# A rank behind the next batch's first scores, its counts in 16 bits, a norm ahead of a context half, and a semaphore of its own for the router's matrix

## The reference, cut to what matters

```python
x = x + tanh(g_xattn) * (gelu(layernorm(x) @ ctx.T) @ ctx)       # per batch
xf = layernorm(x)                                                  # the "second norm"
scores = softmax(xf @ gate_w)                                      # gate_w: the router's matrix, 512 x 8
top_scores, top_idx = top_k(scores, 2)
for each expert e:  xs = scale[:, e] * xf                          # scale: top_scores, 0 elsewhere
    y += (silu(xs @ w1[e]) * (xs @ w3[e])) @ w2[e]
x = x + tanh(g_ffn) * y
```

## Time and profile before

| | us |
|---|---|
| median of 3 runs | 810.37 |
| lowest and highest | 801.66, 811.13 |
| the profiled execution | 810.19 |
| its span | 808.4 |

### The profile page before, as it was taken

The page is one execution under the profiler, slowest core; times in us unless marked ns, Lnnn a source line. Parts: engine busy times, 40 slices in busy tenths (PEclk is TensorE's granted clock), DMA queues, the critical chain, the costliest instruction groups (busy, mean ns, idle before and its releaser), DMA issues.

```text
span 808.4 us, 17787 instructions
## 1 busy us (share of the span) xinstructions
PE 679.2 (84%) x4670; PEld 471.4 (58%) x4671; DVE 427.3 (53%) x1281; ACT 465.0 (58%) x775; POOL 424.2 (52%) x662
## 2 busy tenths in 40 slices
PE   0598897988898897888878734999999999999992
PEld 0576676876677776767767632555554555555551
DVE  2247667567676677676766772333334333333331
ACT  3777787587686877876867421443443443443441
POOL 2333356456457555764675652455555555555552
PEclk9999999699999999989999956999999999999997
DMA  5325545525444354355441222467566666566564
GB/s 160 103 77 171 147 133 138 151 90 136 141 138 114 115 170 122 123 147 170 121 121 49 72 73 66 79 107 127 106 116 115 108 113 117 106 108 124 99 114 75
DMA packets 51344, 94.30 MB, mean 117 GB/s; under 512 B 17024, under 2 KB 25344, under 8 KB 51312
## 3 DMA queue, kind: packets, MB, share of 16 engines
q1 hardware_dynamic: 34096, 60.02, 26.9%
q0 software_dynamic: 16400, 33.89, 22.8%
q10 hardware_dynamic: 816, 0.02, 0.1%
HBM read 61.89 MB, written 32.01 MB: 116 GB/s over the span
## 4 chain that ended last, share of the span: by engine, by line
DMA 29%; issue 16%; PE 14%; POOL 12%; DVE 7%; ACT 5%; POOLq 1%; DVEq 1%; ACTq 0%; SPq 0%; another core or an unknown queue 0%
DMA out_rows<-ctx_raw,meta 24%; PE bank L1173 4%; PE bank L1304 3%; PE bank L1161 2%; POOL route_table L470 2%; DMA ctx_raw<-xf_rows,meta 2%; ACT squares L571 2%; DVE stats L796 2%; POOL ex L462 2%; PE bank L1314 2%; DMA w_raw<-in_L_ffn_w 2%; POOL out_rows L540 1%; POOL exp_f L437 1%; DVE xf L871 1%; POOL ve L429 1%
## 5 line engine op out<-in xcount | busy, mean ns | idle before, releaser
L1304 PE MATMUL bank<-w,ctxT 128*128 x756 | 174.5, 381 | 0.0
L540 POOL DMA_INDIRECT out_rows<-ctx_raw,meta x63 | 99.3, 1577 | 123.9 <-DMA out_rows<-ctx_raw,meta 109.4
L1173 PE MATMUL bank<-ctx_part,a_part 125*112 125x512 f16 x576 | 145.5, 401 | 10.1 <-DVE a_part L828 10.1
L1161 PE MATMUL bank<-xnT,ctxT 128*125 128x224 f16 x1152 | 131.6, 275 | 4.7 <-DVE xnT L849 2.3
L1161 PEld LDWEIGHTS bank<-xnT,ctxT 128*125 128x125 f16 x1152 | 122.5, 148 | 6.2 <-issue 4.7
L1304 PEld LDWEIGHTS bank<-w,ctxT 128*128 128x128 f16 x756 | 74.3, 98 | 76.1 <-issue 1.6
L609 ACT ACTIVATE ctxT<-bank 128x1000 f16<-128x1000 f16 x96 | 95.4, 1014 | 22.2 <-PE bank L1119 22.0
L1173 PEld LDWEIGHTS bank<-ctx_part,a_part 125*112 125x112 f16 x576 | 75.7, 137 | 54.7 <-issue 8.3
L773 ACT ACTIVATE ctxT<-bank,cols 128x256 f32<-128x256 f32 x63 | 29.9, 474 | 112.6 <-issue 102.4
L1314 PE MATMUL bank<-w2s,ctxT 128*128 x378 | 91.9, 379 | 1.3 <-DVE ctxT L1079 1.3
L528 POOL DMA_INDIRECT ctx_raw<-xf_rows,meta x66 | 65.4, 991 | 29.5 <-issue 19.2
(11 more groups left out here) (142 smaller groups left out, 1078.1 us busy)
## 6 DMA issues: line engine op xcount, KB each, us to landing
ctx_raw<-in_ctx SPq DMA_DIRECT2D x48, 448.0 KB
w_raw<-in_L_ffn_w SPq DMA_DIRECT2D x24, 512.0 KB
x<-in_x SPq DMA_DIRECT2D x16, 448.0 KB, 5.6
out_rows<-x SPq DMA_DIRECT2D x16, 448.0 KB, 4.7
xf_rows<-xf SPq DMA_DIRECT2D x16, 448.0 KB
ctx_raw<-in_ctx SPq DMA_DIRECT2D x48, 52.0 KB
meta<-route_table SPq DMA_DIRECT2D x66, 1.0 KB
ctx_raw<-xf_rows,meta POOLq DMA_INDIRECT x66
```

Source lines behind the costliest of these rows:

```text
L540: g.indirect_dma_start(out=out, out_offset=bass.IndirectOffsetOnAxis(ap=meta[n][:, 0:1], axis=0), in_=y_sb[n % 2], in_offset=None, compute ...
L1161: ins = t_.matmul(dst, ctxT[u][:, hc * KD + k, c * CS:c * CS + CR], xnT[u][:, hx, k, :], start=j == 0, stop=j == KD * len(PARTS) - 1)
L1173: ins = t_.matmul(O_ps[t][0:TT, :], a_part[ha][:, c, t * TT:(t + 1) * TT], ctx_part[u][hc][:, c, :], start=c == 0 and (ha, hc) == PARTS[0] ...
L1304: ins = t_.matmul(H_ps[u][:, :], rows, w, start=m == 0, stop=m == KD * len(PARTS) - 1)
```

## The change

Four edits.

1. `small_loaded` becomes two semaphores, `g_loaded` for the gates and `gate_loaded` for the router's matrix. ScalarE waits only for the gates, TensorE only for the matrix.
2. `lower`, M and R are float16 instead of float32, and a second, 16-bit array of ones is made at the start.
3. On TensorE `rank(i-2)` no longer ends the step of batch i. It is the second item of the step of batch i+1, right behind the first `scores` (the last batch keeps one more at its old place). On VectorE `route_pos` moves along: from the end of a step to the place ahead of the first `a_low` of the next.
4. On VectorE the middle of a step is reordered. It was: routing scores, second context half, weight's low part, second `a_low`, `norm2`. It is: weight's low part, second `a_low`, `norm2`, second context half, routing scores.

```diff
-        lower = sb("lower", [TT, TT])
+        lower = sb("lower", [TT, TT], F16)
...
+        ones16 = sb("ones16", [TT, P], F16)
...
-        M = sb("M", [TT, 2, E])
-        R = sb("R", [TT, 2, E])
+        M = sb("M", [TT, 2, E], F16)
+        R = sb("R", [TT, 2, E], F16)
...
-        small_loaded = sem("small_loaded")
+        g_loaded, gate_loaded = sem("g_loaded"), sem("gate_loaded")
...
+            seq.done(g.memset(ones16[:, :], 1.0))
...
             for n, g in enumerate((g_xattn, g_ffn)):
-                a.dma_start(g_raw[:, n:n + 1], g.rearrange("(a n) -> a n", a=1).to_broadcast([P, 1])).then_inc(small_loaded, 16)
-            a.dma_start(gate[:, :, :], gate_w.rearrange("(k p) e -> p k e", p=P)).then_inc(small_loaded, 16)
-            act.wait_ge(small_loaded, 48)
+                a.dma_start(g_raw[:, n:n + 1], g.rearrange("(a n) -> a n", a=1).to_broadcast([P, 1])).then_inc(g_loaded, 16)
+            a.dma_start(gate[:, :, :], gate_w.rearrange("(k p) e -> p k e", p=P)).then_inc(gate_loaded, 16)
+            act.wait_ge(g_loaded, 32)
...
                 if not u and later(i, 1):
                     stats2(j)
+                if later(i, 3):
+                    route_pos(i - 3, w, h - 1 - w)
                 a_low(i, u, 0)
...
                     context_factors(i + 1, w)
-                if later(i, 3):
-                    route_scores(i - 3, w)
-                if not last:
-                    context_low(i + 1, w, 1)
                 late_matrix(weight_low, i, u, h)
                 a_low(i, u, 1)
                 if later(i, 1):
                     norm2(j)
+                if not last:
+                    context_low(i + 1, w, 1)
+                if later(i, 3):
+                    route_scores(i - 3, w)
...
                     xnT_low(i + 1, i * 4 + 3, w, 1)
-                if later(i, 2):
+                if last:
                     route_pos(i - 2, u, h - 1)
...
-            pe.wait_ge(small_loaded, 48)
+            pe.wait_ge(gate_loaded, 16)
...
                 scores(i, u, 0)
+                if later(i, 3):
+                    rank(i - 3)
...
                     trans_ctx(i + 1, w, 5)
-                if later(i, 2) and not last:
-                    rank(i - 2)
```

More of the change, by code:

```diff
@@ L1203, in rank @@
                 t_.matmul(rk_ps, lower[:, :], M[:, :, :].rearrange("p t e -> p (t e)"), start=True, stop=False)
-                t_.matmul(rk_ps, ones[0:TT, 0:TT], R[:, :, :].rearrange("p t e -> p (t e)"), start=False, stop=True).then_inc(rank_made, 1)
+                t_.matmul(rk_ps, ones16[:, 0:TT], R[:, :, :].rearrange("p t e -> p (t e)"), start=False, stop=True).then_inc(rank_made, 1)
             trans_ctx(0, 0, 0)
@@ L1270, in _ @@
             pe.wait_ge(pos_read, B)
-            t_.matmul(cnt_ps, ones[0:TT, :], R[:, 0, :], start=True, stop=True).then_inc(counts_made, 1)
+            t_.matmul(cnt_ps, ones16[:, :], R[:, 0, :], start=True, stop=True).then_inc(counts_made, 1)
             pe.wait_ge(w_split, 3 * E)
@@ L1347 @@
 POOL_IDENT = 6
-POOL_START = 16
+POOL_START = 17
 _INS = ['x', 'ctx_1024', 'g_xattn', 'g_ffn', 'L0_ffn_gate_w', 'L0_ffn_w1', 'L0_ffn_w2', 'L0_ffn_w3']
```

## The result

The changed kernel takes **824.08 us**, median of four runs (820.33 to 825.87); the kernel before took 806.01 beside it (four runs, 800.43 to 811.13). The ratio is 1.0233 [1.0187, 1.028]: 1.9 to 2.8% slower, where I had forecast 821 us and 1.3% (and had given 0.76 to a change of less than 2%, which this interval neither shows nor rules out). The profiled execution took 825.45 us with a span of 823.5, against 810.19 and 808.4.

A forecast was written before the change was run, and what follows sets the result against it. VectorE, though busy only 53%, was taken to set the pace where nothing covers its added work. On 810.19 us: -6.2 + 6 x 1.2 + 6 x 1.1 + 2.9 = +10.5, so 820.7, forecast 821; eight in ten 807 to 831.

The forecast's parts named there:

- Part 1: Start-up: with its own semaphore for the matrix, ScalarE's tanh and what follows come 6.2 us earlier; other end 4.4.
- Part 2: Odd batch's end: moving the rank leaves TensorE's stall, now waiting for xnT; gain 0.06 us per odd batch.
- Rival D: TensorE's clock falls more often in longer idle pieces, one more fall per pair of batches; 831 us, slower, chance 0.19.
- Part 3: Positions behind the residual delay VectorE's chain and TensorE's logits; +1.2 us per odd batch, 0 per even batch.
- Part 4: Even batch: later routing scores delay the next statistics, +1.1 us; xf stall shrinks by 1.2, xn stall grows to 3.0.
- Part 5: Last batch: positions and later routing scores delay GpSimd's sends and exponential, so the last residual comes 2.9 us later.
- The sign that I had set: Time from one even batch's scores to the next's: 53.8 us before, 56.1 forecast; 54 or less would refute it.
- B: Rival: only the start counts, the later edits cost nothing; 804 us, chance 0.15.
- A: Rival: one of the two per-batch costs, the even one, is covered by other waits; 812 us, chance 0.12.
- C: Rival: TensorE's own order is the bound, so its waits for R and xf vanish; 785 us, chance 0.04.

The follow-up runs named there:

- e1: Kernel before with only the semaphore split between gates and router's matrix; 803.83 us, ratio 0.9929 to the kernel before.
- e6: Changed kernel with odd batches' positions back in the even batch's end and routing scores back ahead of the weight's low part; 808.55 us, ratio 1.0037 to the kernel before.
- e2: Changed kernel with the rank (still 16-bit) and all positions back at the end of a batch; 811.31 us, ratio 1.0049 to the kernel before.
- e10: e6 plus 14 idle matmuls on TensorE in the idle piece at each odd batch's end; 808.39 us, ratio 1.0003 to the kernel before.
- e3: Changed kernel with the routing scores put back ahead of the weight's low part; 821.77 us, ratio 1.0163 to the kernel before.
- e5: Changed kernel with only the odd batches' positions moved back to the end of the even batch ahead; 813.71 us, ratio 1.0123 to the kernel before.
- e12: Kernel before with the split semaphore plus 14 idle matmuls ahead of the rank at its old place; 798.13 us, ratio 0.9887 to the kernel before.
- e4: Changed kernel plus 20 idle matmuls ahead of the odd batches' logits; 821.18 us, ratio 1.0136 to the kernel before.
- e8: e6 with even batches' late weight half put last on ScalarE and VectorE, second context half moved ahead; 796.44 us, ratio 0.9824 to the kernel before.

## Why the prediction was right, and where its sizes were off

It had the sign and the mechanism, and 824.08 lies well inside 807 to 831. That it lies so near to 821 is luck in part. I added +10.5 us to a profiled execution of 810.19, and the kernel before had a median of 806.01 beside the change. The change itself cost 18 us by medians and 2.3% by ratio (1.9 at least), where I had 10.5 us and 1.3%; in the two profiles it is 11.9 up to the expert part and 15.1 in all. So the sum was too small, and a base that was 4 us too high made up for part of it.

**Part 1, the start: -6.2 forecast, -6.38 in the profile, -5.7 for the edit alone.** The context rows were there in time, which had been the doubt.

**Part 2, the rank: the stall renamed, gain 0.06.** As forecast: 3.28 to 3.29 us where it was 2.64 and the rank. In how often slow scores follow little changed, four of six in both profiles (three in e1, five in the change's second profile). Whether the longer piece has a price of its own stays open. In e6 slow scores followed six times of six, and each odd batch took 29.3 us, 1.5 more than the four of e2 with fast scores; the filler (e10) took just that 1.5 us off each odd batch. But behind the same piece slow scores followed three times of six in e3 and three of four in e5. Over all profiles it is 30 of 40 against 9 of 15, which is 0.15 of 1.5 us per odd batch, 1.4 us in all, if it is no accident. Rival D named the lengthening, without a price of its own. The rank alone was not moved in a run.

**Part 3, the positions: +1.2 forecast per odd batch, +2.87 in the pair shown (22.07 to 24.94), +2.3 on the mean of six.** This is the term that was mis-sized. Both halves of the mechanism are there. The block stands unbroken between residual and a_low, and the logits wait for pos_read, 2.23 us where I had reckoned 2.6. What I priced at nothing was the clock behind that wait. The logits end late by the wait and by their own 0.7 us, and the attention takes 5.35 us instead of 2.79; it was slow in all six odd batches (4.46 to 5.35), in five of six in the second profile. I had supposed that a slower TensorE is hidden in its own waits, since VectorE sets the pace. For the kernel before that holds: its odd batches with fast scores at the end took 27.9 us with an attention of 4.31 and 27.6 with one of 2.79, and VectorE never waited for a there. In e12 the same attention was slow in four (4.47 to 4.48) of the five odd batches with fast scores, and they took 27.8 to 27.9 us where the one with a fast attention took 27.7. In the change the attention starts 1.8 us later behind the residual (344.65 - 340.70 against 340.78 - 338.65) and is longer still, and the cover is used up. VectorE's next inputs pass through TensorE and ScalarE. ScalarE and VectorE in that odd batch:

```profile
350.62 1.91 ACT L611 ACTIVATE ctxT<-bank 128x1000 f16<-128x1000 f16 x2 [5.76 <-PE bank L1123]
```

```profile
355.55 0.68 DVE L830 SCALAR_TENSOR_TENSOR a_part<-a_f,factors,a_part 125x448 f16<-125x448 f32 x1 [1.89 <-ACT a_part L625]
```

ScalarE waits for the transposes behind the slow attention, and VectorE waits 1.89 us for ScalarE, as it does in five of the six odd batches (1.88 to 1.89). About 1.6 us of the excess gets through, and e4 gave back just that (31.1 to 29.5). So this is rival D's mechanism, in the odd batches, on top of the forecast. The Trainium skill's rule that I had weighed ("TensorE: Matmul & The Clock Gate", section "HAM oscillation — how this bites in real kernels") says that the price of waits for data between short bursts is paid in every repetition. The traces agree nearly for the odd logits, 17 of 18 in the change's two profiles and e3, and less for the scores at an odd batch's end, four of six in the change and 30 of 40 over all.

**Part 4, the even batch: +1.1 forecast, +1.25 in the pair.** Statistics, batch and next norm are late by that much, and e3 gave 1.0 back on that chain. The split into 0.8 for xf and 3.0 for xn did not hold in this pair: TensorE waited 1.86 and 1.23, since a slow attention between them (4.44 us) had used up the second wait. Elsewhere the waits for xn reached 2.9. On the mean of the five even batches it is only +0.4, because the profile before has one even batch of 31.1 us; against e1's 26.7 it is +0.6.

**Part 5, the last batch: +2.9 and one even term of 1.1 forecast from the totals of batch 14 on, 3.4 measured** (12.9 less 9.6). The sends wait 2.91 us for the routing scores and the exponential follows them, as foreseen:

```profile
464.26 1.06 POOL L472 DMA_INDIRECT route_table<-route,pos_i  x1 [2.91 <-DVE tok L916]
...
469.19 2.94 POOL L464 TENSOR_TENSOR ex<-euler,dl 112x16 f32<-112x16 f32 x1
```

```profile
472.17 0.17 DVE L907 TENSOR_REDUCE sm<-ex 112x2 f32<-112x16 f32 x1 [2.50 <-POOL ex L464]
```

**The sum.** Forecast +10.5; in the profiles +11.9 at the first gather and +15.1 at the end. The last 3.2 us lie within the scatter of the expert part (317.3 to 320.6). The 1.4 us up to the gather are small because the errors partly met: 1.1 too little in each of six odd batches (7), 0.7 too much in each of five even batches (3.5), 0.6 too much at the last batch, and 1 that went again between the last residual and the gather. A total near the forecast does not prove the terms. The sign that I had set, the pair at 56.1 us, came out at 57.95.

**Rivals.** B is refuted: e2 and e5 show that the moved positions and rank cost 9 to 15 us. A's time is refuted too; its mechanism, the even term covered, held in part, since 0.4 to 0.6 us of 1.1 show on the mean. C is refuted by the waits. D happened in part. By my own sign (slow scores and attentions clearly more than before) it did: the loop's scores and attentions took 26 us longer in all than at the higher clock, 17 in the kernel before and 15 in e4. But three of the six slow attentions had been there before, and only some 1.6 us per odd batch reached the chain.

**Left open.** Why the weight's transfer takes 9 us in some batches and 5 in others; the longest even batches of nearly every profile (28.8 to 34.7 us) are ones in which it took 7.2 us or more, and it decides how much any shortening here brings. What separates e5 from e2, and e6 from e1. Why the filler adds nothing to e8. The order of norm2 and the context half, and the 16-bit counts, were not tried by themselves.

## What to carry to other kernels

Before moving small work out of the way of a busy engine, find where the engine that really sets the pace waits, and put the work into that wait: the same 1.2 us of positions cost nothing that shows at their old place and some 2.3 us per odd batch outside it. Check every semaphore that comes with the block; the engine that waits for it pays twice when its clock falls in the wait. A slow stretch that is covered today can come to light when the work ahead of it moves back by a microsecond. And look at what is first in the queue of the engine that waits longest: taking the weight half out of the way of a gelu and a context part (e8) brought 12 to 17 us, nearly as much as the four edits together cost.

## What the runs showed of the hardware

- Idle pieces of TensorE of 1.8 to 2.25 us before the odd logits were followed by an attention of 4.46 to 5.35 us instead of 2.78 in 17 cases of 18 (the change 6 of 6, its second profile 5 of 6, e3 6 of 6), the matmuls running at the lower of the clock's two levels (1.2 and 2.4 GHz) for part or all of it. With the idle matmuls in the same place none of six was.
- Shorter pieces can do the same. Pieces of 1.0 to 1.25 us right before that attention were followed by a slow one (4.08 to 4.48 us) in 14 cases of 24 (the kernel before 3 of 6, e1 4, e2 2, e12 5). Pieces of 1.07 to 1.17 us ahead of the rank (e2) were followed by scores of 2.51 three times of three; there matmuls shortly before the piece had been slow already.
- Idle pieces of 3.2 to 3.3 us before the scores were followed by slow scores 30 times of 40 (4 and 5 of 6 in the change's two profiles, 6 of 6 in e6). In the change's profile the matmuls of the last 6 us before a fall and before none are the same, and so is the wait's length; what decides I can't tell from these rows.
- In the executions whose clock was kept up at one place other stretches were slow (e4, e10); whether they were moved there or only scatter is not shown. A local gain of 1.6 us per odd batch, some 10 us in all, became 3 to 8 us in e4, and one of 1.5 became nothing that can be told in e10.
- The transfer of a 512 KB weight in this loop took from 4.6 to 9.1 us in one execution (e10), read where ScalarE waits for it.
- The 16-bit rank took 0.17 us for each matmul where the 32-bit one was 0.37 for two passes, and the 16-bit counts took VectorE as long as the 32-bit ones (0.15 to 0.17 us): the narrow type bought nothing on VectorE.
